# GpSimd takes three of eight sets of query-key products, VectorE reads its five from PSUM, and units run in another order

## The reference

```python
# block 1: dilated 3x3 neighbourhood attention, 4 dilations (1, 2, 4, 8), 32 channels = 2 heads of 16 for each
qkv = einsum('bchw,oc->bohw', gn(x), w_qkv).reshape(B, 3, nd, bd, H, W)
for i, dil in enumerate(DILATIONS):
    attn = einsum('bhdn,bhdkn->bhnk', qh, unfold3x3(k, dil)) * scale     # 9 scores for a pixel and head
    attn = softmax(attn, axis=-1)
    outs[i] = einsum('bhnk,bhdkn->bnhd', attn, unfold3x3(v, dil))
gate = softmax(gn(x).mean(axis=(2, 3)) @ w_gate.T + b_gate)              # a weight for each image and dilation
x = x + concatenate([outs[i] * gate[:, i] for i in range(nd)])
# block 2: channel attention, 4 heads of 32 channels, q = k = v = p
p = einsum('oc,bchw->bohw', W_qkv, gn(x)) + b_qkv
att = softmax(einsum('bhdn,bhen->bhde', p, p) * hw ** -0.5)
x = x + einsum('oc,bchw->bohw', W_proj, att @ p) + b_proj
```

## Time and profile before

| | |
|---|---|
| runs | 86.25, 83.36, 85.00 us: median 85.0 |
| profiled execution | 84.24 us |
| its span, first to last instruction | 82.4 us |
| around the span | 1.84 us |
| busy PE / DVE / ACT / POOL | 68.5 / 67.3 / 29.4 / 41.4 us |
| granted TensorE clock, mean | 0.994 |

### The profile page before, as it was taken

One profiled execution on the slowest core, in us unless ns is written; L12 is line 12 of the kernel. 1 busy time (PEld: TensorE's weight loads), 2 busy tenths in 40 slices (PEclk: granted clock), 3 DMA queues, 4 the chain that ended last, 5 costly groups with the idle time before them and its releaser, 6 DMA issues.

```text
span 82.4 us, 2430 instructions
## 1 busy us (share of the span) xinstructions
PE 68.5 (83%) x988; PEld 49.5 (60%) x988; DVE 67.3 (82%) x183; ACT 29.4 (36%) x92; POOL 41.4 (50%) x84
## 2 busy tenths in 40 slices
PE   0469999579995699899979879679999999999960
PEld 0449854257882359566768654368677768566530
DVE  1322899999699998999999699889999998587860
ACT  1942655954367000000020001240795362765210
POOL 7103208918600007999999999699992004200000
PEclk9999999999999999999999999999999999999997
DMA  1981047000000000000000000000000000002253
GB/s 25 313 230 70 0 94 166 5 0 0 8 0 4 0 12 0 0 0 0 4 8 0 0 0 0 0 0 8 0 0 0 8 0 8 4 35 92 79 176 127
DMA packets 3195, 3.04 MB, mean 37 GB/s; under 512 B 368, under 2 KB 3056, under 8 KB 3184
## 3 DMA queue, kind: packets, MB, share of 16 engines
q1 hardware_dynamic: 2896, 2.63, 11.3%
q10 hardware_dynamic: 288, 0.26, 0.9%
HBM read 1.84 MB, written 1.05 MB: 35 GB/s over the span
## 4 chain that ended last, share of the span: by engine, by line
DVE 44%; PE 27%; POOL 12%; issue 5%; DMA 5%; ACT 2%; SPq 1%; POOLq 0%
PE ps L807 25%; DVE pv L635 12%; DVE qk L594 9%; DMA cs<-consts_dram 5%; POOL rstd L332 4%; POOL acc L369 3%; DVE acc L647 2%; DVE pv L647 2%; DVE x L666 2%; DVE prob L614 2%; DVE smax L601 2%; DVE ssum L611 2%; POOL pv L369 2%; DVE sums L562 1%; POOL pexp L346 1%
## 5 line engine op out<-in xcount | busy, mean ns | idle before, releaser
L807 PE MATMUL ps<-prob,sel 64*128 64x192 f32 (+6 forms) x192 | 17.8, 313 | 2.7 <-DVE pv L635 1.6
L635 DVE TENSOR_TENSOR pv<-ps,v 128x128 f32<-128x128 f32 (+7 forms) x32 | 17.1, 568 | 1.8 <-PE ps L807 0.8
L807 PE MATMUL ps<-xn,wp 128*32 128x256 f32 (+1 forms) x208 | 17.3, 386 | 0.8 <-ACT q L409 0.7
L807 PEld LDWEIGHTS ps<-prob,sel 64*128 64x128 f32 x192 | 13.7, 186 | 6.9 <-DVE pv L635 3.5
L807 PE MATMUL ps<-xt 128*128 128x128 f32 x60 | 11.7, 337 | 3.3 <-DMA xt<-x_dram 3.3
L369 POOL TENSOR_TENSOR pv<-pv 128x240 f32<-128x240 f32 (+3 forms) x24 | 14.1, 595 | 0.5 <-DVE pv L635 0.5
L332 POOL TENSOR_TENSOR rstd<-gvar,mhalf 128x2 f32<-128x2 f32 (+1 forms) x6 | 4.8, 808 | 16.3 <-DVE gvar L540 16.3
L807 PEld LDWEIGHTS ps<-xn,wp 128*32 128x32 f32 (+1 forms) x208 | 9.9, 117 | 5.2 <-ACT xn L435 1.2
L369 POOL TENSOR_TENSOR acc<-acc,pv 128x256 f32<-128x256 f32 (+4 forms) x20 | 12.7, 637 | 0.5
L807 PEld LDWEIGHTS ps<-xt 128*128 128x128 f32 x60 | 9.6, 232 | 4.6 <-DMA xt<-x_dram 3.3
L594 DVE TENSOR_TENSOR qk<-q,k 128x672 f32<-128x672 f32 (+7 forms) x21 | 11.5, 608 | 0.7 <-ACT k L412 0.7
(11 more groups left out here) (81 smaller groups left out, 90.3 us busy)
## 6 DMA issues: line engine op xcount, KB each, us to landing
out_dram<-x SPq DMA_DIRECT2D x8, 128.0 KB, 1.7
xt<-x_dram SPq DMA_DIRECT2D x2, 256.0 KB, 4.7
xt<-x_dram ACTq DMA_DIRECT2D x2, 128.0 KB, 2.8
xt<-x_dram SPq DMA_DIRECT2D x2, 128.0 KB, 2.6
sel<-selc_dram SPq DMA_DIRECT2D x4, 64.0 KB, 2.3
wp<-wpack_dram SPq DMA_DIRECT2D x1, 194.0 KB, 4.4
wp<-wpack_dram SPq DMA_DIRECT2D x1, 131.0 KB, 2.6
cs<-consts_dram SPq DMA_DIRECT2D x2, 64.0 KB, 3.5
```

Source lines behind the costliest of these rows:

```text
L635: last = nc.vector.tensor_tensor(o, a, b, ALU.mult)
L807: return nc.tensor.matmul(o, w, m, start=start, stop=stop)
```

## The change

GpSimd multiplies query and key of units (0,3), (1,2) and (1,3), from SBUF. VectorE keeps (0,0), (0,1), (0,2), (1,0) and (1,1), and reads their queries in PSUM; before, three of its eight units did. The scores are summed in another order, the value tiles of the later units are projected later and in pairs, and three PSUM banks instead of five take the early tiles. The second transfer that SP issues is now the group matrix, and four runs of `keep_clock` in the middle are gone; sums and squares are taken in the images' new order of arrival. The places of the inverse roots among GpSimd's additions are unchanged.

The core of the diff (transfers, GpSimd, VectorE, TensorE, in this order):

```diff
+ARRIVAL = (0, 2, 6, 4, 1, 3, 5, 7)
...
-        PROJ_BANKS = (0, 1, 2, 3, 6)
+        PROJ_BANKS = (0, 1, 6)
+        VALUE_BANKS = (4, 5)
...
-        Q_IN_PSUM = [(0, 0, 0)] + [(0, s, PHASES - 1) for s in range(2, ND)]
+        Q_AT = {(0, 0): 512 * 5, (0, 1): 512 * 2, (0, 2): 512 * 3, (1, 0): 512 * 2, (1, 1): 512 * 3}
+        DVE_PRODUCTS = list(Q_AT)
+        POOL_PRODUCTS = [(0, 3), (1, 2), (1, 3)]
+        SUM_ORDER = [(0, 0), (0, 1), (0, 3), (0, 2), (1, 0), (1, 2), (1, 1), (1, 3)]
...
+            load_x(0)
             sp.dma_start(cs[:, C_GRP:C_GRP + P], consts[:, C_GRP:C_GRP + P]).then_inc(grp_loaded, 16)
+            load_x(2)
...
+            def multiply_qk(ph, s):
+
+                pool.wait_ge(proj_copied, max(copied_by(0, s, ph), copied_by(1, s, ph)))
+                if ph:
+                    pool.wait_ge(scores_ready, summed(0, s))
+                for ci in range(3):
+                    for o, a, b in query_operands(ph, s, ci):
+                        last = nc.gpsimd.tensor_tensor(o, a, b, ALU.mult)
+                last.then_inc(pool_qk_ready, 1)
+
+            multiply_qk(0, 3)
             pool.wait_ge(nbias_ready, PHASES)
...
+            multiply_qk(1, 2)
 
             pool.wait_ge(gexp_ready, 1)
...
             nc.gpsimd.tensor_tensor(gate[:], gsel[:], grec[:], ALU.mult).then_inc(gate_ready, 1)
+            multiply_qk(1, 3)
...
-            gate_shift()
-            multiply_qk(0, 2, 2)
+            gate_shift()
+            multiply_qk(1, 0, 2)
+            softmax_shift(0)
+            softmax_divide(0)
             for i in range(3):
-                multiply_qk(0, 3, i)
...
                 multiply_qk(1, 1, i)
-            for i in range(2):
+            for i in range(3):
                 multiply_pv(0, 0, i)
...
+            gate_logits()
+            sum_scores(0, 3)
+            sum_scores(0, 2)
...
             spread(0, 0, 1)
-            keep_clock(3)
             spread(0, 0, 2)
...
+            for i in range(2):
+                spread(1, 2, i)
             restore(0)
-            spread(1, 1, 1)
-            group_stats(0)
+            spread(1, 2, 2)
             restore(1)
+            for i in range(2):
+                spread(1, 3, i)
+            group_stats(0)
+            spread(1, 3, 2)
+            group_stats(1)
```

More of the change, by code:

```diff
@@ L463, in _ @@
             square_sum(7)
-            for n in range(1, 3):
+            for n in range(1, 4):
                 copy_tile(n)
@@ L835, in project, with wait_norms @@
+            def wait_norms(ph):
+                for j in range(SLOTS):
                     b = PHASES * j + ph
-                    if n == 0 or tiles[n - 1][2] != ph:
-                        every = [PHASES * i + h for h in range(PHASES) for i in range(SLOTS)]
-                        same = [x for x in every if (x in NORM_ON_ACT) == (b in NORM_ON_ACT)]
-                        pe.wait_ge(xn_act_ready if b in NORM_ON_ACT else xn_ready, same.index(b) + 1)
-                    last = mm(ps[32 * j:32 * j + 32, bank, 0:N], wp[:, w0:w0 + CD], xn[:, b, :])
@@ L842, in project @@
-                last.then_inc(proj_ready, 1)
+                    every = [PHASES * i + h for h in range(PHASES) for i in range(SLOTS)]
+                    same = [x for x in every if (x in NORM_ON_ACT) == (b in NORM_ON_ACT)]
+                    pe.wait_ge(xn_act_ready if b in NORM_ON_ACT else xn_ready, same.index(b) + 1)
+            def project(n):
+                if n >= EARLY:
+                    pe.wait_ge(prob_ready, 1)
+                    if n >= EARLY + 4:
+                        pe.wait_ge(proj_copied, EARLY + 2)
+                elif n >= len(PROJ_BANKS):
+                    pe.wait_ge(proj_copied, n - len(PROJ_BANKS) + 1)
+                project_to(copy_source(n), *tiles[n]).then_inc(proj_ready, 1)
@@ L863, in sum_scores @@
                 if s == 0 and ph:
-                    pe.wait_ge(proj_copied, len(tiles))
+                    pe.wait_ge(proj_copied, EARLY)
                     pe.wait_ge(gshift_ready, 1)
@@ L1028, in _ @@
             sum_scores(1, 1)
-            keep_clock(1)
+            spread(0, 1, 1)
+            sum_scores(1, 3)
             spread(0, 1, 2)
+            for n in range(EARLY + 2, EARLY + 4):
+                project(n)
             spread(0, 2, 0)
-            sum_scores(1, 2)
-            keep_clock(1)
+            for n in range(EARLY + 4, EARLY + 6):
+                project(n)
             for i in range(1, 3):
                 spread(0, 2, i)
-            sum_scores(1, 3)
-            for i in range(2):
+            for i in range(3):
@@ L1038, in _ @@
                 spread(0, 3, i)
-            keep_clock(2)
-            spread(0, 3, 2)
-            keep_clock(6)
-            for i in range(3):
-                spread(1, 0, i)
-            spread(1, 1, 0)
-            restore(0)
-            spread(1, 1, 1)
-            group_stats(0)
-            restore(1)
-            spread(1, 1, 2)
-            group_stats(1)
+            for s in range(2):
+                for i in range(3):
+                    spread(1, s, i)
             for i in range(2):
@@ L1062, in _ @@
                 transpose(0, i)
-            for i in range(1, 3):
-                spread(1, 3, i)
             transpose(1, 0)
```

201 lines of the change are left out of this document (101 added, 100 removed).

## The result

The changed kernel takes 93.73 us (median of four runs, 93.2 to 95.61), 1.122 times the kernel before, 95% interval 1.105 to 1.138. The prediction was 88.9 us with 83.6 to 91.3: slower as forecast, but by 12% in place of 5.5%, and outside the range. Some executions of a kernel run over 1.5% longer than its fastest one, and ratios leave these out.

A forecast was written before the change was run, and what follows sets the result against it. No engine bound it throughout; VectorE's queue was followed most (44% of the span). Attention behind the late `nbias` moved `sum_second` from 64.34 to 69.0, adding 4.7 us to 84.24: 88.9 us, range 83.6 to 91.3.

The forecast's parts named there:

- the clock as a rival of 1 to 2 us: Ahead of the first `prob`, TensorE's clock falls and spreads take up to twice 0.92 us; part of a 0.14 rival.
- The removed `keep_clock` matmuls save nothing: Unread matmuls taken out in the middle ran in TensorE's idle time, so removing them gains no time.
- (0,3) and (1,2) on GpSimd: Query-key products moved to GpSimd take 3.0 and 4.3 us, priced from its additions.
- GpSimd's small instructions: On the way to the first `prob`, those formerly blocked by VectorE's port use take 0.2 us each.
- VectorE idle ahead of `prob`: VectorE waits 3.2 us for `gate`, which stands behind GpSimd's products of unit (1,2).
- phase 1's first product: After phase 0's value products, phase 1 starts at 45.5 us, against 46.96 before.
- last product ends: Phase 1's value products, with unit (1,3) and both variances, end at 57.85 us.
- additions and `nbias`: VectorE's eight additions beside GpSimd's take 5.4 us from 57.85; `nbias` behind them ends at 63.6.
- The start, 0.4 of gain: Constants issued second let the group sums start earlier; `nbias` of phase 1 ends at 13.2 instead of 13.6 us.
- hand-overs close up: Turns between TensorE and VectorE cost nothing beyond VectorE's work: 0.5 us less, 83.7 us; chance 0.20.
- VectorE's queue decides: Only the wait for `gate` costs; VectorE's queue gets shorter: 2.5 us less, 81.7 us; chance 0.19.
- Slower still: GpSimd's products cost a third more, or TensorE's clock falls, on the way to `prob`: 90 to 92 us; chance 0.14.

The follow-up runs named there:

- `fill_start`: The changed kernel with two more unread matmuls around the first statistics; median 93.74 us, ratio 1.122 to the kernel before.
- `fill_more`: `fill_all` with 30 instead of 20 unread matmuls ahead of block 2's projections; median 91.46 us, ratio 1.085.
- `fill_all`: The changed kernel with unread matmuls (fillers) added at the start, in the middle and ahead of block 2's projections; median 91.99 us, ratio 1.098.
- `bias_early`: `fill_all` with the variance ahead of unit (1,3)'s value products, `nbias` ahead of VectorE's additions, and 18 end fillers; median 87.1 us, ratio 1.040.
- `before_bare`: The kernel before without its seven runs of `keep_clock` between phase 1's scores and block 2's projections; median 85.15 us, ratio 1.013.
- `tuned`: `bias_early` with unit (1,2)'s GpSimd products behind the gate, inverse roots behind other additions, and 9 end fillers; median 83.76 us, ratio 1.000.
- `tuned_start`: `tuned` with the kernel before's order of transfers and of the images' sums; median 83.06 us, ratio 0.993.

## Why the prediction was wrong: the clock as a rival of 1 to 2 us, and what it left out of the hand-overs

The failed step, as the prediction put it: "The removed `keep_clock` matmuls save nothing: they ran in TensorE's idle time", with the clock left to a rival of 0.14 and "1 to 2 us". They had kept that idle time from costing something. Removing them and adding waits let the clock fall three times; all fillers together give back 3.0 us by the ratios, their own price taken off. How much of this is the removed matmuls and how much the new waits isn't separated; in the kernel before their removal alone cost 1.3%. In the profile: `sum_second` is at 73.5 in `fill_start`, and at 70.4 in `fill_more` once its late start is taken off (71.89, less 1.52 at `nbias` of phase 1, 14.96 against 13.44). The prediction had read the fall of the clock behind TensorE's last matmul and counted one new gap. It had three: ahead of `prob`, among the last spreads of phase 0, and between `group_stats` and the projections, the 6.7 us of which its own sum implied. The Trainium skill, "TensorE: Matmul & The Clock Gate", section "HAM oscillation — how this bites in real kernels", tells of a kernel in which TensorE's wait for a transfer in every turn of a loop puts it on the lower level, so that the next matmuls start cold. Here the rows agree in kind, for waits on other engines: the third fall alone made 2.17 us of projections into 3.78.

Step by step, on `fill_all` and `fill_more`, where the clock is full:

| step | forecast | measured |
|---|---|---|
| (0,3) and (1,2) on GpSimd | 3.0, 4.3 | 3.10, 4.34 |
| GpSimd's small instructions | 0.2 | 0.20 |
| VectorE idle ahead of `prob` | 3.2 | 2.9 |
| first `prob` ends | 28.6 | 28.7 |
| second `prob` ends | 40.9 | 41.0 |
| phase 1's first product | 45.5 | 46.8 |
| first residual | 52.35 | 53.9 |
| last product ends | 57.85 | 60.4 |
| additions and `nbias` | 5.75 | 4.9 |
| from there to `sum_second` | 5.4 | 5.3 |

- **The parts up to the second `prob` were right**, to 0.1 us; so was the price of GpSimd's multiplications, taken from its additions, and that `gate` decides. The 0.1 has some luck in it: `nbias` of phase 1 came 0.5 late (13.67 in `fill_all` against 13.2), and TensorE's way from there to the scores was 0.3 shorter than forecast, the gate's seven instructions 0.1.
- **From there to phase 1, 1.3 us too little, and most of it the fillers'.** Chain of waits of `fill_all`:

```profile
41.88 3.90 PE ps L829 x39
45.78 1.06 issue
...
52.50 3.90 PE ps L829 x51
```

  TensorE is followed from 41.88 without a break, but 1.0 us of these 3.90 are the four fillers shown above. Without them the first product would come at 45.8 by the changed kernel's rows (3.8 after the second `prob`, and 1.0 from spread to product), so about 0.3 is left of the 1.3. The value tiles are done before 41.88. The stretch from 52.5 has no fillers: TensorE is the chain there for unit (1,2), `restore` and the spreads of (1,3), where the forecast followed VectorE; that makes 0.25.
- **From the residuals to the last product, 1.0 too little.** `gsq` and `gvar` of group 1 take 0.67 and 0.62 beside GpSimd's additions where 0.16 was assumed: the port was counted for the big instructions, and not for these two, which have VectorE's next product behind them.
- **The additions, 0.85 too much.** The eight took 4.3 us, not 5.4: 0.65 to 0.82 when blocked, 0.34 when not, and GpSimd stood in its inverse root part of the time. In `bias_early` they took 5.1.
- **The start, 0.4 of gain that did not exist.** The bound was put at "TensorE at 5.33 or the late image", and the late image took all of it; besides, the late constants of the earlier trace rows weren't there in the two other traces with these transfers. In the sum it weighs little: `nbias` of phase 1 ends at 13.4 to 13.8 against 13.2.

At full clock these make 69.0 + 1.3 + 0.25 + 1.0 - 0.85 - 0.1 = 70.6, with the fillers in it; `fill_more` has 70.5 when its start is set to that of the kernel before (71.89, less 1.35 for 14.96 against 13.61). That is 6.2 us above 64.34; the ratio of `fill_more` says 7.2. The likely reason is the profiled execution of the kernel before: 84.24 us, with group sums that start 0.8 later than those of `before_bare`, where later sets of that kernel have medians of 83.75 (19 executions) and 83.65 (17). Without the fillers' 1.0 the steps would end at 69.5, against the forecast 69.0. So the order was forecast to 0.5 us in sum, in part by luck, since the 1.0 too little and the 0.85 too much cancel; the larger part of the miss is the clock.

**The rivals.** That hand-overs close up, and that VectorE's queue decides, are refuted by the 2.9 us ahead of `prob` and by 1.085 at full clock. "Slower still", at 0.14, was the case that came, with the clock and not GpSimd's price: 3.0 us by the ratios, some 4 by the estimate above, where 1 to 2 were priced. The result, 93.7, lies above its 90 to 92. It was also joined to the wrong case: a falling clock doesn't compete with the forecast; it adds to it.

**What the order costs.** The two steps which the prediction named as its price are confirmed by taking each back: the products ahead of `gate` 2.4 to 3.6 points, `nbias` behind the additions 4.5 to 5.7 (against `fill_more` and `fill_all`), and with both gone 1.6% is left, which the new places of the inverse roots and fewer fillers take away. The price of `nbias` is rather too low, since the 18 fillers of `bias_early` held the projections. What VectorE saves (18 products, 5.1 us) is hardly seen in the time even so: with these waits mended, `tuned` is at 1.000. The eight fillers of the middle are still in it. In `tuned_start` TensorE has the chain for 45%, VectorE for 33%.

## What to carry to other kernels

When an edit removes unread matmuls or opens a gap on TensorE, list each new gap, and price for each what follows it at half the clock, up to the place where the clock came back in the trace; add this to the forecast rather than setting it against it. If fillers are to close a gap, count their own time wherever something waits behind them. When work moves to another engine, look first at what small chain stands behind it in that queue (here seven instructions of 0.2 us up to `gate`), and put the move behind the chain. A result that opens a long way through several engines (`nbias`) goes ahead of bulk work of the same engine, even if that work is awaited too.
